# Gated linear attention with experts on one core: the states of chunks 1 and 2 as three fp32r products

## What is computed

```python
q, k, v = rope(xn @ Wq.T), rope(xn @ Wk.T), xn @ Wv.T      # 4 heads share one k and v
dt = softplus(xn @ Win.T + dt_bias); G = cumsum(dt * A)     # within a chunk
xc = v * dt
y_intra = ((q @ k.T) * decay) @ xc                          # per chunk
cstates = (k * exp(Glast - G)).T @ xc                       # per chunk, 128x128 per head
state   = state * exp(Glast) + cstates                      # over the 4 chunks
y_inter = (q * exp(G)) @ previous_state
y = rmsnorm(y_intra + y_inter) * silu(xn @ Wg.T) @ Wo.T
```

## Time and profile before

| | us |
|---|---|
| median of 3 runs | 2097.31 (2096.49 to 2097.52) |
| profiled execution, its own time | 2098.08 |
| its span, first to last instruction | 2096.3 |
| PE busy in the span | 1980.6 (94%) |
| DVE busy | 1616.7 (77%) |
| ACT busy | 1135.6 (54%) |
| POOL busy | 872.9 (42%) |

### The profile page before, as it was taken

One profiled execution on the slowest core, in us unless ns is written; L12 is line 12 of the kernel. 1 busy time (PEld: TensorE's weight loads), 2 busy tenths in 40 slices (PEclk: granted clock), 3 DMA queues, 4 the chain that ended last, 5 costly groups with the idle time before them and its releaser, 6 DMA issues.

```text
span 2096.3 us, 32088 instructions
## 1 busy us (share of the span) xinstructions
PE 1980.6 (94%) x9216; PEld 1504.0 (72%) x9216; DVE 1616.7 (77%) x2937; ACT 1135.6 (54%) x2379; POOL 872.9 (42%) x705
## 2 busy tenths in 40 slices
PE   5799999999999999989899999999999999998992
PEld 3577777777777777767677777777777777677881
DVE  5877777777777777767977777777777777748995
ACT  5455555555555555542455555555555555537881
POOL 1243443434343434343354444444444444434661
PEclk9999999999999999999999999999999999999996
DMA  7222121212121212135121212121212121228778
GB/s 254 100 58 59 48 61 49 60 46 64 42 68 38 71 37 71 39 93 187 42 71 41 70 36 70 40 69 36 70 40 70 40 70 40 77 70 295 229 231 321
DMA packets 147515, 182.05 MB, mean 87 GB/s; under 512 B 12935, under 2 KB 89319, under 8 KB 147454
## 3 DMA queue, kind: packets, MB, share of 16 engines
q1 hardware_dynamic: 137310, 155.52, 25.5%
q0 software_dynamic: 8704, 25.21, 3.4%
q10 hardware_dynamic: 1440, 0.58, 0.1%
HBM read 152.90 MB, written 28.37 MB: 86 GB/s over the span
## 4 chain that ended last, share of the span: by engine, by line
PE 86%; DVE 5%; DMA 2%; issue 2%; ACT 2%; POOL 1%; SPq 0%; ACTq 0%; DVEq 0%; POOLq 0%
PE PJ L1228 14%; PE PJ L1230 14%; PE PJ L1229 14%; PE OU L1228 5%; PE OU L1229 5%; PE OU L1230 5%; PE SC L1363 5%; PE CS L1373 4%; PE YE L1384 4%; PE YI L1228 2%; PE YI L1229 2%; PE YI L1230 2%; PE TR L1311 1%; PE OU L1325 1%; PE TR L1228 1%
## 5 line engine op out<-in xcount | busy, mean ns | idle before, releaser
L471 POOL TENSOR_TENSOR zl<-yb,zh 128x512 fp32r<-128x512 f32 x122 | 157.8, 1294 | 309.9 <-ACT zh L977 309.9
L757 POOL TENSOR_TENSOR gm<-gbc,amask 128x512 f32<-128x512 f32 x128 | 180.7, 1412 | 202.4 <-DVE wfl L1859 175.8
L1228 PE MATMUL OU<-woh,zh 128*128 128x512 f32 x488 | 227.1, 465 | 2.0 <-POOL zl L471 2.0
L1228 PE MATMUL PJ<-xnh,wgh 128*128 128x512 f32 x512 | 221.3, 432 | 3.6 <-POOL wgl L727 3.6
L1228 PE MATMUL PJ<-xnh,wqh 128*128 128x512 f32 x544 | 219.7, 404 | 3.0 <-DVE qh_f L1778 1.8
L1230 PE MATMUL PJ<-xnh,wql 128*128 128x512 f32 x544 | 212.7, 391 | 0.0
L1229 PE MATMUL PJ<-xnl,wqh 128*128 128x512 f32 x544 | 212.7, 391 | 0.0
L1789 DVE SCALAR_TENSOR_TENSOR gm<-SC,hcoef,gm 128x128 f32<-128x128 f32 x512 | 144.2, 344 | 78.1 <-PE SC L1363 74.4
L1230 PE MATMUL PJ<-xnh,wgl 128*128 128x512 f32 x512 | 203.1, 397 | 0.0
L1229 PE MATMUL PJ<-xnl,wgh 128*128 128x512 f32 x512 | 202.8, 396 | 0.0
L977 ACT ACTIVATE zh<-yb 128x512 fp32r<-128x512 f32 x122 | 76.6, 628 | 230.0 <-PE OU L1230 161.2
(11 more groups left out here) (553 smaller groups left out, 5357.9 us busy)
## 6 DMA issues: line engine op xcount, KB each, us to landing
gbc<-decay_exponents SPq DMA_DIRECT2D x128, 256.0 KB, 4.8
stage<-in_wq SPq DMA_DIRECT2D x72, 256.0 KB, 3.4
stage<-in_wg SPq DMA_DIRECT2D x64, 256.0 KB, 2.6
stage<-in_wo SPq DMA_DIRECT2D x64, 256.0 KB, 2.6
gbc<-in_wm SPq DMA_DIRECT2D x48, 256.0 KB
stage<-in_wkv SPq DMA_DIRECT2D x34, 256.0 KB, 2.6
experts<-in_wm SPq DMA_DIRECT2D x16, 512.0 KB, 6.3
experts<-expert_rows SPq DMA_DIRECT2D x16, 512.0 KB, 14.5
```

What stands on the lines that cost most here:

```text
L471: nc.gpsimd.tensor_tensor(lo[:], yb[:, c, :], hi[:].bitcast(F32), ALU.subtract).then_inc(S["zlo"], 1)
L757: g.tensor_tensor(gm[:, c % 2, :].rearrange("p (h i) -> p h i", h=HG), gbc[:, c % 2, :].rearrange("p (h i) -> p h i", h=HG), amask[:].unsq ...
L1228: nc.tensor.matmul(out_, a_hi, b_hi, start=first, stop=False)
```

## The change

- `key_rows` on ACT writes chunk 0 in float32 as before and chunks 1 and 2 as the high part `knh`, in two copies instead of one.
- DVE makes `knl` for chunks 1 and 2 in one subtraction out of `TR` and `knh` (`key_rows_lo`): ahead of `rope(3, 0)`, in the very first step behind it.
- `weighted(1)` and `weighted(2)` write to a buffer of their own, `vwx` (the second half of `t2`), and wait for the last reader of it, DVE, and no longer for the chunk state ahead.
- ACT copies `vwx` to `vwh` (`weighted_hi`): for chunk 1 behind the decays of round 0, for chunk 2 ahead of the decays of round 1. Each copy waits for the chunk state ahead.
- DVE subtracts `vwl = vwx - vwh` at the end of rounds 0 and 1, behind `gated(c + 1)` and ahead of `wfl` of the next round.
- PE makes the states of chunks 1 and 2 with `mm3` of `knh`, `knl`, `vwh`, `vwl`, behind the product with the state and no longer ahead of it.

```diff
                         def weighted(c):
-                            if c:
-                                at.wait("cstate", c)
+                            if c == 0:
+                                at.wait("vhi", 1)
+                            elif c == 1:
+                                at.before("vwlo", 2)
                             else:
-                                at.wait("vhi", 1)
+                                at.wait("vwlo", 1)
+                            out_ = vwx if c else vwf
                             for h in range(HG):
-                                ins = a.activation(vwf[:, h * P:(h + 1) * P], vf[:, c * P:(c + 1) * P], ACT.Copy,
+                                ins = a.activation(out_[:, h * P:(h + 1) * P], vf[:, c * P:(c + 1) * P], ACT.Copy,
                                                    scale=head(2, c, h))
+                        def weighted_hi(c):
+                            at.wait("cstate", c)
+                            at.wait("vw", c + 1)
+                            a.activation(vwh[:], vwx, ACT.Copy).then_inc(S["vwhi"], 1)
...
-                            a.activation(knf[:], TR[:, 0:3 * P].rearrange("p (a b) -> p a b", a=3),
+                            a.activation(knf[:, 0, :], TR[:, 0:P], ACT.Copy)
+                            a.activation(knh[:, 1:3, :], TR[:, P:3 * P].rearrange("p (a b) -> p a b", a=2),
                                          ACT.Copy).then_inc(S["kn"], 1)
...
+                                if c == 1:
+                                    weighted_hi(2)
                                 decay(c + 1)
+                                if c == 0:
+                                    weighted_hi(1)
...
                             if c == 0:
                                 at.wait("kn", 1)
                                 at.before("stt", 3)
+                                ins = nc.tensor.matmul(CS[:], knf[:, c, :], vwf[:], start=True, stop=True)
                             else:
                                 at.wait("stt", c)
-                            nc.tensor.matmul(CS[:], knf[:, c, :], vwf[:], start=True, stop=True).then_inc(S["cstate"], 1)
+                                at.wait("knlo", 1)
+                                at.wait("vwlo", c)
+                                ins = mm3(CS[:], knh[:, c, :], knl[:, c, :], vwh[:], vwl[:], True, True)
+                            ins.then_inc(S["cstate"], 1)
...
                         for c in range(NCH):
+                            if c:
+                                inter(c)
                             if 0 < c < 3:
                                 chunk_state(c)
-                            if c:
-                                inter(c)
...
+                        def key_rows_lo():
+                            at.wait("kn", 1)
+                            at.before("cstate", 3)
+                            v.tensor_tensor(knl[:, 1:3, :], TR[:, P:3 * P].rearrange("p (a b) -> p a b", a=2),
+                                            plain(knh[:, 1:3, :]), ALU.subtract).then_inc(S["knlo"], 1)
...
+                            if c < 2:
+                                at.wait("vwhi", c + 1)
+                                if c == 0:
+                                    at.before("cstate", 3)
+                                else:
+                                    at.wait("cstate", 2)
+                                v.tensor_tensor(vwl[:], vwx, plain(vwh[:]), ALU.subtract).then_inc(S["vwlo"], 1)
```

More of the change, by code:

```diff
@@ L166, in build @@
         states = [st, sthf, stlf]
+        vwx = t2[:, 1, :]
         rmsh, rmsl = ql[:, 0, :], ql[:, 1, :]
@@ L308, in build @@
             proj=10, tr=2, score=4, cstate=3, yinter=3, yintra=4, ssq=1, spread=1, oproj=4,
-            vraw=1, vhi=1, kn=1, dec=4, expg=3, vw=3, whi=4, tanh=4, ysq=4,
+            vraw=1, vhi=1, kn=1, dec=4, expg=3, vw=3, vwhi=2, whi=4, tanh=4, ysq=4,
             rsln=1, rms=1, rmshi=1, zhi=4,
             coef=1, roperd=5, rope=5, wsc=4, wlo=4, stt=3, yt=3, y=4, gated=4, u=4, z=4, accd=4,
-            vlo=1, gmask=4, zlo=4, rmslo=1,
+            vlo=1, gmask=4, zlo=4, rmslo=1, knlo=1, vwlo=2,
         )
@@ L1830, in step @@
                             rope(3, 0)
+                            key_rows_lo()
                             decays_c(1)
```

## The result

The changed kernel takes 2113.21 us in the median of 5 runs (2111.6 to 2116.25), the kernel before beside it 2097.52 (2096.49 to 2102.56). The ratio on record is 1.0066 (the quotient of the two medians would be 1.0075), with a 95% interval of 1.0051 to 1.0081: slower, clear of the noise. The profiled execution took 2115.01, with a span of 2113.2.

What follows compares the result with a forecast made beforehand. PE, busy 94% of the span, was taken to bound the kernel. Terms -10.0 + 9.8 + 2.0 + 3.6 + 6.0 + 0.7 = +12.1 on 2098.08 gave 2110.2, less 0.8 for the median: 2109.4 us, range 2097 to 2119.

Steps and rivals of the forecast that it cites:

- The passes, -10.0: PE's chunk states: three passes replace the float32 product, saving 0.15 to 0.16 us per state, two states in 32 steps.
- The hold in `b` = 1, +9.8: Round 0 of `b` = 1: POOL's second subtraction holds `vwl`, PE waits 0.6 to 0.65 us in each of 15 steps.
- The first rival: The `vwl` subtraction is not held by POOL, both `b` = 1 terms go: 2097.6 us, no change; chance 0.13.
- Round 1 of `b` = 1, +2.0: POOL's next pair waits for loads and comes late in six of 15 steps, costing 0.2 to 0.6 us each.
- The very first step, +3.6: First half's first step, no output projection as cover: PE waits 1.8 us for `vwl` in each of two rounds.
- The second half's first step, +6.0: Two waits for `vwl`, +3.0 us, plus `knl` ahead of `rope(3)` delaying DVE and the scores, +3.0 us.
- the clock, taken as 0 within 0 to 6.6: PE's lower clock level behind the four new 1.8 us waits: 0 to +6.6 us possible, 0 taken.
- The second step of the second half, +0.7: POOL leads there and PE waits for `zl`; POOL comes 0.52 us later and hides one saving.
- The third rival: Long waits lower the clock, or round 1 holds `vwl` 0.6 in all 15 steps: +6.6 or +7, 2116 us; chance 0.13.
- the second (low parts always ready): Rival: low parts are ready whenever PE asks, so PE shows its full saving: 2087.3 us, faster; chance 0.06.

Runs made afterwards that it cites:

- run 8: Changed kernel with the passes reading high parts only and DVE's low-part subtractions kept on 8 columns each; 2093.20 us, ratio 0.9972.
- run 9: Changed kernel with `vwl` ahead of `gated`, `knl` behind the last rotation, float32 states plus three unused 8-column DVE subtractions in first steps; 2091.20 us, ratio 0.9968.
- run 1: Kernel before with only PE's order changed: product with the state ahead of the float32 chunk state; 2102.83 us (one run).
- run 3: Changed kernel with ACT's copy for chunk 1 behind the high parts of the two weights in `b` = 1; 2110.08 us, ratio 1.0053.
- run 11: Kernel before with three additions on 8 unused columns in DVE's first step of each half; 2098.07 us (one run).
- run 10: Changed kernel with `vwl` ahead of `gated` and `knl` behind the last rotation, low parts made in every step; 2097.02 us, ratio 0.9989.
- run 4: Changed kernel with DVE's `vwl` subtraction ahead of `gated` instead of behind it; 2099.68 us, ratio 0.9997.
- run 2: Changed kernel without low parts: the three passes read high parts only, DVE's subtractions removed, ACT's extra copy kept; 2103.41 us, ratio 1.0014.
- run 7: Changed kernel with `vwl` ahead of `gated`, `knl` behind the last rotation, and float32 states in each half's first step; 2111.47 us, ratio 1.0064.
- run 6: Changed kernel with float32 states of chunks 1 and 2, without low parts, in each half's first step; 2118.04 us, ratio 1.0098.

## Why the prediction was right, point by point

The forecast was 2109.4 with a range of 2097 to 2119; 2113.2 was measured. The mechanisms held; that the sum came out so near is partly luck, as said at the end. The terms, read as differences of distances between chunk states:

- **The passes, -10.0.** Right. A step without new waits is 52.80 and not 53.13: 0.33, predicted 0.31. Runs 8 and 9 show it bare, in 27 inner steps each. The swap of the order costs nothing (run 1).
- **The hold in `b` = 1, +9.8.** Right in mechanism and in size. 14 waits of 0.60 and two of 0.70 (the second step of each half) are 9.8; the prediction had 15 of 0.65 and gave the second half's second step a term of its own. The Trainium skill (SBUF — State Buffer, section Who interferes with whom) has a vector instruction with two SBUF inputs and a GpSimd instruction that reads SBUF exclude one another; the trace agrees, with 32 ends at 0.55 behind POOL's. The first rival (not held, after the Mode Summary of Advanced Engine Details and Errata) is refuted by these 32, and run 3 shows by moving POOL alone that the wait is POOL's.
- **Round 1 of `b` = 1, +2.0.** Right in kind, too large: the waits sum to 1.4, of 0.1 to 0.3 in seven steps, and 0.71 in the second step of the second half.
- **The very first step, +3.6.** The step is 3.97 longer, so its waits cost 4.3. What was missed: POOL's `gm` runs there too, from 107.97, and held the second `vwl` to 1.22, so that the second wait is the longer one.
- **The second half's first step, +6.0.** The term that was most too small: 7.8, and the step that failed is the clock, taken as 0 within 0 to 6.6. The keys cost 3.7 (4.02 more to its first `CS`, less 0.60 of hold in the step ahead, plus 0.31 of saving), predicted 3.0. Of them 2.3 is the longer wait, 5.90 against 3.56, and 1.0 the twelve passes behind it, which took 5.19 to `CS` and not 4.21, at the lower level for longer. The wait also stands elsewhere than predicted: at the gate projection, which waits for a rotation to have read `PJ`, not at the scores. The waits for `vwl` cost 4.1, predicted 3.0, of which 1.3 can be the clock by an estimate from rounded figures, and at most, since PE waits for a part of the slow time. Run 1 warns not to lay the 1.0 to the change alone: it has no low parts, and its twelve passes took 5.26 too. The windows from one first `CS` to the next (length, busy times, clock), before and after, are these; with the low level at half speed, 0.06 x 58.29 - 0.04 x 54.51 = 1.3 us:

```profile
993.36:1047.87 54.51, 47.51 (x207) 34.84 (x205) 48.37 (x91) 26.54 (x57) 15.89 (x11) 0.96 0.19 55
```

```profile
1003.44:1061.73 58.29, 48.31 (x209) 35.63 (x207) 49.62 (x95) 27.81 (x60) 15.83 (x11) 0.94 0.15 37
```

- **The second step of the second half, +0.7.** Wrong: it was 0.07 shorter than before, though it has two waits of 0.7 for `vwl`. The wait for `zl` grew to 2.47 as expected, but the lower clock behind it was gone: from 1066 to 1085 us the granted clock is 1.00, while 1.65 us had been lost to it before. Nor is this an effect of the change: run 11, whose loop is that of the kernel before, had a clock of 1.00 there too, and run 10, with low parts, had not. Runs 9 and 10 have the same wait for `zl` there (3.1) and take 56.2 and 58.8 for this step; when the clock falls stays open.

With all terms the length should have grown by about 12, and it grew by 12.46. That the two agree so well is luck: errors of up to 1.8 in one direction and 0.8 in the other partly cancel, and kernels that do the same work differ by 3.6 in this length (1701.09 to 1704.73), for the most part through the clock around the change of halves. The profiled runs differ by another 4.4 outside the loop, where no mechanism was found, and where those of one kernel and the next differ by up to 6. The third rival (clock, or longer holds in round 1) had both its parts touched, with 1.3 of 6.6, and in round 1 with waits of up to 0.3 and not 0.6 in all steps; the second (low parts always ready) is refuted by the 21 waits of the view, but runs 4 and 9 show that an order in which they are ready exists.

**What the expectations missed** was the code. In run 2 the step that failed was the silent assumption that taking instructions away from DVE leaves the rest in place. Shown: edits of DVE's program alone switch it on and off (2 against 8, whose pages count 2937 and 3033 instructions of DVE, and 7 against 9, with 3027 and 3033 and the same computation in the loop). With it queue 14 moves 30 packets against 1 in the first half's loop, DVE stands idle at the start of six passes, and a pass costs 1.6 us more in run 2 and up to 4.2 in run 7. Only argued: that the idle time is the loading of code, and that a page's edge is crossed. The Trainium skill (Runtime: NRT & Kernel Launch, section Instruction fetch mechanics) says that a taken branch to code outside the two pages that are held makes the engine load it before it goes on. The packets and the idle time behind the loop's branch agree with that; no run shows where the pages lie, and runs 7 and 9 differ in their waits of the first step besides its instructions.

## What to carry to other kernels

A saving on the bounding engine is worth what its operands' last link allows: here 10 us of passes were paid back more than twice, through subtractions that stood on VectorE behind an operation with an unrelated wait, or ahead of one that others needed; moved by one place each, they cost nothing in the loop. Look at such an edit step kind by step kind, since a half's first steps, without other work as cover, cost as much as all the others together. And when an edit changes how many instructions lie ahead of or in a loop, compare the packets of the instruction queues before any theory on semaphores; a version of this kernel with the same loop was 20 us slower with 64 packets than with 33. The best one here (run 9) is 0.9968 of the kernel before, with an interval of 0.9958 to 0.9979, and 22 us under the changed kernel.

## What the runs showed of the hardware that was not expected

- VectorE can stand idle for 1.8 to 3.7 us at the start of each pass of a loop, most likely while its code is loaded; the profile shows it as "issue" (1.83 in run 2) or puts it down to a releaser that was long done (3.48 in run 7). The sign is the packets of queue 14: 63 or 64 in a run and 30 in the first half's loop (runs 2, 6 and 7), against 32 to 34 and 0 or 1 in all others.
- Between two POOL operations in a row, the held VectorE operation can get its turn: started 0.22 behind POOL's first, `vwl` took 1.62 and POOL's pair 2.99 for 2.54 (run 4). Started in the second, it took 1.52 and ended 0.54 behind POOL (changed kernel). It does not always get its turn: one `vwl` of the changed kernel was held for 5.01 us, through four operations of POOL in a row. What tells the two cases apart, no run shows.
- TensorE's granted clock differed between runs of the same work around the change of halves: at the same place one run lost 1.65 us to the lower level and another had 1.00 throughout (run 11).
